# A two-layer transformer tower on one core: fp16 operands turned by DMA alone, three gathers for tile 1, new bank plan and new orders

## What is computed

```python
h = word_emb[ids] + pos_emb[pos] + type_emb[type];  h = layernorm(h) * gamma + beta
h = h + relu((performer(layernorm(h)) @ Wo.T + bo) @ Wfc.T + bfc)
h = h + prototype_ffn(layernorm(h))      # top 2 of 32, gates from distances
h = h + rope_attention(layernorm(h))     # causal, 16 heads of 16
h = h + relu(layernorm(h) @ Q(W1).T + b1) @ Q(W2).T + b2     # Q: ternary
```

## Time and profile before

| | us |
|---|---|
| three runs | 488.57, 484.67, 488.35 |
| median | 488.35 |
| profiled execution | 489.89 |
| its span | 488.2 |

### The profile page before, as it was taken

The page is one execution under the profiler, slowest core; times in us unless marked ns, Lnnn a source line. Parts: engine busy times, 40 slices in busy tenths (PEclk is TensorE's granted clock), DMA queues, the critical chain, the costliest instruction groups (busy, mean ns, idle before and its releaser), DMA issues.

```text
span 488.2 us, 11666 instructions
## 1 busy us (share of the span) xinstructions
PE 396.0 (81%) x3872; PEld 266.8 (55%) x3901; DVE 366.1 (75%) x1009; ACT 276.7 (57%) x589; POOL 246.4 (50%) x332
## 2 busy tenths in 40 slices
PE   3271757677868798999999988899999998898976
PEld 1140434435555556666666666666666675655634
DVE  4455488989788689889897879688978796765552
ACT  1223565254747385948585858485765747364531
POOL 6854226365747475757675657474654524342000
PEclk9775557589999899999999999999999999999999
...
GB/s 113 238 46 247 189 32 88 11 66 54 92 133 106 93 105 130 117 141 150 126 181 105 171 131 148 170 103 117 158 112 153 126 136 97 127 44 77 66 44 77
DMA packets 176860, 56.34 MB, mean 115 GB/s; under 512 B 168416, under 2 KB 174208, under 8 KB 176800
## 3 DMA queue, kind: packets, MB, share of 16 engines
...
## 4 chain that ended last, share of the span: by engine, by line
PE 32%; issue 13%; DVE 12%; DMA 11%; POOL 6%; ACT 5%; SPq 3%; DVEq 0%; ACTq 0%; POOLq 0%
PE PS L1322 9%; DMA hgT<-hgs 4%; PE PS L1751 3%; PE PS L1885 3%; PE PS L1619 3%; DMA qkT<-qs 3%; PE PS L1384 3%; DMA xTo<-xso 2%; PE PS L1867 2%; DVE split L989 1%; PE PS L1332 1%; DMA rTm<-split 1%; SPq L458 1%; PE PS L1333 1%; PE PS L1493 1%
## 5 line engine op out<-in xcount | busy, mean ns | idle before, releaser
L989 DVE TENSOR_REDUCE split<-PS 128x16 f16<-128x2048 f32 x16 | 36.7, 2297 | 7.9 <-PE PS L1716 7.8
L1332 PE MATMUL PS<-proj_hi,qkT 128*128 128x176 f16 x128 | 24.8, 256 | 18.7 <-DMA qkT<-qs 13.7
L588 POOL TENSOR_TENSOR stage_f<-stage_f 128x512 f32<-128x512 f32 x16 | 20.3, 1269 | 29.0 <-DVE stage_f L977 16.9
L581 POOL TENSOR_TENSOR rstdR<-rstdR,consts 128x1 f32<-128x1 f32 x16 | 8.7, 545 | 51.7 <-DVE rstdR L954 51.7
L1867 PE MATMUL PS<-w1q,xTM 128*128 128x512 f16 x128 | 32.9, 379 | 0.8 <-DVE xTM L1028 0.6
L1885 PE MATMUL PS<-w2q,mT 128*128 128x256 f16 x256 | 30.6, 273 | 1.7 <-ACT mT L1074 0.9
L1619 PE MATMUL PS<-faT_hi,hgT 128*128 128x256 f16 x128 | 26.2, 292 | 5.7 <-DMA hgT<-hgs 5.6
L1077 ACT ACTIVATE ehat<-esum,nmeanE,rstdE 128x256 f32<-128x256 f32 x16 | 9.5, 595 | 37.6 <-DVE nmeanE L770 22.0
L1885 PEld LDWEIGHTS PS<-w2q,mT 128*128 128x128 f16 x256 | 24.3, 98 | 6.0 <-issue 1.9
L1332 PEld LDWEIGHTS PS<-proj_hi,qkT 128*128 128x128 f16 x128 | 13.4, 105 | 24.2 <-DMA qkT<-qs 16.4
L598 POOL TENSOR_TENSOR rstdM<-rstdM,consts 128x1 f32<-128x1 f32 x16 | 8.8, 550 | 33.3 <-DVE rstdM L1016 33.3
...
## 6 DMA issues: line engine op xcount, KB each, us to landing
...
rT<-split SPq DMA_TRANSPOSE x26, 3.3
```

The lines of the kernel that those rows point to most:

```text
L588: g.tensor_tensor(rot[:, :, :].rearrange("p h d -> p (h d)"), rc[:, :], rs[:, :], ALU.add).then_inc(rot_ok, 1)
L989: v.tensor_reduce(slots(48)[:, 0:H, 0].rearrange("p (c j) -> p j c", j=4), PS[:, BANK["mk1"]:BANK["mk1"] + 4, :].rearrange("p j (c k) -> p ...
L1332: pe.matmul(dst, qkT[:, c0 + c, :], proj_hi[:, :], start=True, stop=False)
```

## The change

Six things change; the arithmetic of each product stays.

1. `BY_PE` shrinks from 28 turns to 7: `P` of tile 0, `o` of 0 and 15, `r` and `M` of 14 and 15. The 21 others go to `DMA_TRANSPOSE`: `o` of 1, 2, 14; `M` and `r` of 0, 1, 2, 13; `rT3.15`; `mT.15`; `rT1` and `rT2` of 0, 14, 15; `hgT` of 0 and 15. The operations of PE, ACT and DVE for fp16 turns (`rT1p`, `rT1a`, `rT1b` and so on) and the semaphore `turn_ok` are gone.
2. Tile 1 gathers from three tables like tile 0. `emb_type` becomes two buffers. The wait for the table `pt` moves from tile 1 to tile 2.
3. `load_w2` is issued behind `qp.0`.
4. New banks: `fQ` has 4 and 5, `fK` 0 and 1; `of`, `y`, `Rtr`, `rqk`, `rv` and `rot_` share bank 7.
5. Matmuls on nothing: one ahead of `m1.15`, six ahead of `m2.15` (the entry for `mk2` has no call that reads it).
6. All numbers of `START`, `STRETCH` and `PLACE` are new, and with them the order of each engine.

```diff
-START = (1.40537, 5.55987, 9.74075, 12.65258, 16.91573, 21.20954, 25.54553, 29.89477, 34.27529, 38.71698, 43.20261, 47.66727, 52.19494, 54.66439, 59.30117, 64.06203)
+START = (15.32428, 21.39685, 27.55784, 28.87087, 35.0305, 41.20738, 47.43255, 53.63816, 59.87893, 66.17932, 72.47996, 78.82444, 85.19901, 88.21914, 94.59957, 101.02611)
-    "sq": (-15.70252, -9.02388, -10.17824), "qT": (-20.94188, -17.2022, -20.19668), "diag": (-13.87668, -8.26036, -8.0608), "fK": (-14.33904, -9.0266, -9.06747),
+    "sq": (-38.70227, -21.84097, -23.62394), "qT": (-30.9939, -18.51016, -17.72932), "diag": (-32.59877, -16.74413, -15.51198), "fK": (-39.64337, -19.98461, -21.10499),
...
-    "qk": 6, "kmxT": 7, "kbc": 7, "fK": 0, "v": 7, "ctx": 2, "fQ": 0, "o": 3,
-    "of": 2, "Ftr": 7, "prt": 1, "fh": 0, "y": 7, "Rtr": 2, "rqk": 2, "rv": 1,
-    "mk1": 3, "pvx": 3, "pvT": 7, "wo": 0, "m1": 4, "m2": 2, "Ptr": 1, "ont": 2,
-    "Mtr": 4, "rot_": 7, "rT3p": 1, "mTp": 3, "rT1p": 0, "rT2p": 4, "hgTp": 6,
+    "qk": 2, "kmxT": 3, "kbc": 4, "fK": 0, "v": 6, "ctx": 3, "fQ": 4, "o": 2,
+    "of": 7, "Ftr": 6, "prt": 0, "fh": 1, "y": 7, "Rtr": 7, "rqk": 7, "rv": 7,
+    "mk1": 3, "pvx": 5, "pvT": 2, "wo": 2, "m1": 0, "m2": 2, "Ptr": 0, "ont": 3,
+    "rot_": 7, "Mtr": 1,
...
 WARM = {
-    "Rtr": {15: 1},
-    "Mtr": {14: 2},
+    "mk2": {15: 2},
     "m1": {15: 1},
-    "m2": {15: 1},
+    "m2": {15: 6},
 }
...
 BY_PE = {
-    "P": (0,), "o": (0, 1, 2, 14, 15), "M": (0, 1, 2, 13, 14, 15),
-    "r": (0, 1, 2, 13, 14, 15), "rT3": (15,), "mT": (15,),
-    "rT1": (0, 14, 15), "rT2": (0, 14, 15), "hgT": (0, 15),
+    "P": (0,), "o": (0, 15), "r": (14, 15),
+    "M": (14, 15),
 }
...
-TERN_BANK = 4
+TERN_BANK = 3
...
-        emb_type = sb("emb_type", [P, D])
+        emb_type = sb("emb_type", [P, 2, D])
...
                 if op == "PT":
...
-                    if t == 1:
-                        load_w2()
...
                     sp.dma_start_transpose(qpT[:, :, :], qe[:, :, :].rearrange("p j n -> p (j n)")).then_inc(qp_ok, 16)
+                    if t == 0:
+                        load_w2()
...
                 wait(g, e2_ok, t - RING + 1)
-                if t == 1:
+                if t == 2:
                     g.wait_ge(ids_ok, 4)
                     g.wait_ge(pt_out, 16)
...
-                          (emb_type[:, :], A["type"].rearrange("(r n) -> r n", n=D), ids[:, 2, t:t + 1]))
-                if t > 0:
+                          (emb_type[:, t % 2, :], A["type"].rearrange("(r n) -> r n", n=D), ids[:, 2, t:t + 1]))
+                if t > 1:
                     tables = (tables[0], (emb[:, slot, :], A["pt"], ids_pt[:, t:t + 1]))
...
-                    wait(g, g_ok[slot], 32 * (t // RING + 1) + (16 if slot == 0 else 0))
+                    wait(g, g_ok[slot], 32 * (t // RING + 1) + (16 if slot < 2 else 0))
+                    if t < 2:
+                        g.tensor_tensor(h_of(t), h_of(t), emb_type[:, t, :], ALU.add).then_inc(g_const, 1)
+                        wait(g, g_const, 24 + t)
                     wait(g, xn_ok["E"], t)
...
-                elif op == "rT1a":
-                    wait(a, turn_ok, TURNS["rT1p", t])
-                    wait(a, s2_ok, t)
-                    copy(rT[:, 0:HP, :][:, 0:4, :].rearrange("p c n -> p (c n)"), halves_of(BANK["rT1p"] + 0)[:, 0:4 * P]).then_inc(rT1_ok, 8)
...
-                elif op == "hgTp":
-                    wait(pe, hgl_ok, t + 1)
-                    wait(pe, gsl_ok, t + 1)
-                    wait(pe, hgh_ok, t + 1)
...
-                    for c in range(9):
-                        last = pe.transpose(halves_of(BANK["hgTp"] + c // 5)[:, c % 5 * P:(c % 5 + 1) * P],
-                                            hgs[:, c * P:(c + 1) * P], ident_h[:, :])
-                    last.then_inc(turn_ok, 1)
```

More of the change, by code:

```diff
@@ L131 @@
     "Ptr": "P", "Pe": "P", "PV": "P", "ont": "o", "oe": "o", "oV": "o",
[3 rows of a table removed]
-    "hgTp": "hgT", "hgTa": "hgT", "hgTb": "hgT",
+    "rot_": "r", "re": "r", "rV": "r", "Mtr": "M", "Me": "M", "MV": "M",
 }
@@ L158, in due @@
     return sorted(((op, t) for op in ENGINE[engine] for t in range(TILES) if taken(op, t)), key=lambda x: (place(*x), x[1]))
-TURNS = {x: n + 1 for n, x in enumerate(y for y in due("PE") if y[0] in ("rT3p", "mTp", "rT1p", "rT2p", "hgTp",))}
 def wait(eng, sem, count):
@@ L812, in step @@
                                            op0=ALU.add, op1=ALU.add).then_inc(qb_ok, 1)
+                elif op == "kmx":
+                    wait(v, fK_ok, t + 1)
+                    wait(v, kmxT_ok, t)
+                    v.tensor_reduce(by_bank(kmx), td(BANK["fK"]), AX_X, ALU.max).then_inc(kmx_ok, 1)
                 elif op == "qd":
@@ L930, in step @@
                         lower_rows("m", 1.0, 16)
-                elif op == "hgTb":
-                    wait(v, turn_ok, TURNS["hgTp", t])
-                    wait(v, y_ok, t)
-                    v.tensor_copy(hgT[:, :, :][:, 5:9, :].rearrange("p c n -> p (c n)"), halves_of(BANK["hgTp"] + 1)[:, 0:4 * P]).then_inc(hgT_ok, 8)
                 elif op == "ws":
@@ L1186, in step @@
                         setup_m()
+                elif op == "onh":
+                    wait(a, on_ok, t + 1)
+                    wait(a, T_ok["o"], 16 * t)
+                    copy(xs["o"][:, 0:D], onorm[:, :]).then_inc(hi_ok["o"], 1)
                 elif op == "Fxn":
@@ L1222, in step @@
                     copy(hgs[:, 0:R2], hg[:, :]).then_inc(hgh_ok, 1)
-                elif op == "hgTa":
-                    wait(a, turn_ok, TURNS["hgTp", t])
-                    wait(a, y_ok, t)
-                    copy(hgT[:, :, :][:, 0:5, :].rearrange("p c n -> p (c n)"), halves_of(BANK["hgTp"] + 0)[:, 0:5 * P]).then_inc(hgT_ok, 8)
                 elif op == "Rxn":
@@ L1242, in step @@
                     copy(slots(16), rot[:, :, :]).then_inc(rh1_ok, 1)
+                elif op == "rh3":
+                    wait(a, rot_ok, t + 1)
+                    wait(a, rT2_ok, 16 * t)
+                    copy(slots(48)[:, H:, :], rot[:, H:, :]).then_inc(rh3_ok, 1)
                 elif op == "rh2":
@@ L1541, in step @@
                     if t == 0:
+                        pe.wait_ge(T_ok["o"], 16)
                         ternary_means()
@@ new lines, in step @@
+                elif op == "rv":
+                    wait(pe, T_ok["R"], t + 1)
+                    free("vr_ok", vr_ok, t)
+                    free("rope_ok", rope_ok, 3 * issued["rqk"])
+                    free("T_r", T_ok["r"], 16 * issued["rot_"])
+                    free("T_R", T_ok["R"], issued["Rtr"])
+                    free("hF_ok", hF_ok, issued["y"])
+                    free("hP_ok", hP_ok, issued["of"])
+                    split_product(PS[:, BANK["rv"], 0:D], "R", "rwv").then_inc(rv_ok, 1)
+                    issued["rv"] = t + 1
```

557 lines of the change are left out of this document (173 added, 384 removed), and 50 rows, old and new, of tables (FOR_DMA, FOR_PE, PLACE).

## The result

| | before | after |
|---|---|---|
| median, us (lowest to highest) | 488.35 (484.67 to 488.57) | 494.99 (493.12 to 498.72) |
| profiled span, us | 488.2 | 495.4 |

The changed kernel is slower: the ratio is 1.0182, 95% interval 1.0147 to 1.0216. The forecast was 487, within 1%.

A forecast was written before the change was run, and what follows sets the result against it. PE was taken to bound the middle, DVE fK.0 to fK.3, dependent chains both ends. −5 + 2 − 1 + 0 − 1.5 + 4.1 = −1.4 us on 488.35 gave 487 (482 to 492; 8 in 10: 475 to 501).

The forecast's parts named there:

- Start, −5: Start to fK.0: w2's move −4, bank split −2.2, GpSimd's gathers +1, taken as −5 us (0 to −7).
- the −4 for w2: Start, wait for qT.0: w2 issued behind qp.0 saves 3.6 us of landing and 0.4 of queue.
- 0, if `kmx.0` meets other DVE work: Start: bound on the −2.2 us from fK.0 no longer waiting for qd.0; nothing won if DVE is otherwise occupied.
- GpSimd's +1: Start: two more gathers ahead of tile 0's Ers, less idle time, cost +1 us (0 to +2.5).
- I let 2 of the 5 us be lost: fK.0 to fK.3, bound by DVE: +2 us of the start's gain lost, net −3 at fK.3 (0 to −8).
- −1 to `y.3`: fK.3 to y.3: M and r turns of three tiles go from PE to DMA, −1 us (0 to −3).
- Steady part, 0: y.3 to fQ.15: same matmuls in another arrangement, 0 us (−10 to +6); wrong if tile spacing moves over 0.4 us.
- The wait on bank 7: Steady part: rv waits for three rope operations reading rqk in the shared bank; five matmul groups should hide it.
- fQ.15 to `y.15`, −1.5: Before y.15: shorter PE queue up to −3.9 us, hgT.15 by DMA +2, taken as −1.5 (−3.9 to +2).
- Tail, +4.1: y.15 to end: rT1/rT2 +2.1, rT3 +1.9, mT +2.1; raw sum +6.1, 2 us hidden: +4.1 (+2.1 to +6.1).
- The transposes are not hidden: Rival: tail +6.1 and hgT.15 +2 in full, start's gain eaten to −1: 495.5 us; chance 0.28.
- The clock falls for the last product: Rival, at m2.15: half clock costs +1.9 us on the middle case, 489; chance 0.1, part of the middle case's.

The follow-up runs named there:

- e4: The kernel before with only the load of w2 moved behind qp.0: 481.68 us, ratio 0.9906 to the kernel before.
- e3: The kernel before with only tile 15's five fp16 turns (hgT, rT1, rT2, rT3, mT) by DMA: 498.33 us, ratio 1.0221 to the kernel before.
- e1: The changed kernel with tile 15's five fp16 turns by PE, placed by hand, one matmul on nothing ahead of m2.15: 495.94 us, ratio 1.0166 to the kernel before.
- e11: e1 with rT1p, rT2p ahead of wo.13, rT3p behind mk2.15, s2.15 ahead of rot_.14: 494.06 us, ratio 1.0253 to the kernel before.
- e18: The kernel before with tile 0's fp16 turns (hgT.0, rT1.0, rT2.0) by DMA: 485.22 us, ratio 0.9984 to the kernel before.
- e9: The changed kernel with the load of w2 back behind PT.1: 494.34 us, ratio 1.0261 to the kernel before.
- e10: The changed kernel with fK.0 waiting for qd.0 again and kmx.0 behind qd.0: 497.83 us, ratio 1.0359 to the kernel before.
- e14: The changed kernel with five start entries moved: qmx.0, qb.0, kmx.0 on DVE, qT.1 on SP, v.1 on PE: 494.85 us, ratio 1.0154 to the kernel before.
- e8: The kernel before with only mT.15 turned by DMA: ratio 1.0067 to the kernel before.
- e17: e8 with six matmuls on nothing ahead of m2.15 in place of one: 488.86 us, ratio 1.0055 to the kernel before.

## Why the prediction was wrong

The forecast by stretch, and what the two profiles show, in us:

| | start to `fK.0` | to `fK.3` | to `y.3` | to `fQ.15` | to `y.15` | to the end | sum |
|---|---|---|---|---|---|---|---|
| forecast | −5 | +2 | −1 | 0 | −1.5 | +4.1 | −1.4 |
| measured | −6.6 | +7.6 | −4.8 | +2.4 | +2.5 | +6.1 | +7.2 |

Up to `y.3` the sum is right (−3.8 for −4), by luck: two misses of opposite sign. The 8.6 us between forecast and result lie behind it, and 6.0 of them in the last two stretches. The step that failed is the price of tile 15's turns by DMA, together with what I credited to PE's shorter queue against it. I had −1.5 and +4.1 for those two stretches, and they were +2.5 and +6.1.

*What bounds the kernel.* Right: PE in the middle, dependent chains at both ends, and nothing won in the middle.

*Start, −5.* Right in its mechanisms, and near in size up to `fQ.0` (−4.1 in the changed kernel, against the −4 for w2). With the bank split on top `fK.0` comes 6.6 us earlier, but `kd.0`, which all of tile 0 hangs on, only 2.8: my condition "0, if `kmx.0` meets other DVE work" came true in another form, since the list has DVE wait for GpSimd ahead of `qmx.0`. GpSimd's +1 was +1.4 on `Pxn.0`.

*"I let 2 of the 5 us be lost", −3 at `fK.3`.* Wrong. `e4` keeps the gain of w2 in the order of before, 0.94% of the time, so that DVE's work did not eat it there. In the changed kernel `fK.3` ended at 124.4, behind the 123 that I had named as the mark of error. I priced the new order by the waits it removes and not by the entries that now stand ahead of a ready instruction; the rows at `qmx.0` and `qT.1` show two such places, and what they are worth at the end is open.

*−1 to `y.3`.* This stretch gained 4.8, more than the 3 I allowed, and made up for the one ahead of it.

*Steady part, 0.* `y.3` to `y.15` went from 272.2 to 277.1 us, 23.1 a tile against 22.7, at the edge of the 0.4 that I had named; 3.0 of these 4.9 are `hgT.15`'s, and the rest is within the spread of single profiles. One piece is sure: `y.3` to `y.5` takes 51.6 us for 45.2 (48.7 to 51.9 in five profiles of the new order with its turns, 43.6 to 46.1 in those of the old one), so that the kernel was 2.6 us late at `y.5`. From there to `y.15` it takes 1.5 us less than before, and although `y.13` ends 7.3 us late, `y.14` is 3.7 and `y.15` 1.1 late. Of the +6.4 up to `y.5`, 3.6 are more idle time of PE, with these waits (us in total, times, longest) where before has 0.3 for `hgT` and none of the other two:

```profile
PE PS L1567 <- DMA rT<-split: 2.8, 2, 1.8
PE PS L1577 <- DMA rTm<-split: 2.2, 2, 1.9
PE PS L1508 <- DMA hgT<-hgs: 1.4, 1, 1.4
```

These turns go by DMA in both kernels; in the new order PE reaches their readers before they land. The other 2.8 are the same 447 matmuls taking longer, at half clock. PE's timeline in the changed kernel ahead of `y.5`:

```profile
209.80 0.62 PE L1567 MATMUL PS<-rT 48*128 48x128 f16 x16 [1.83 <-DMA rT<-split]
210.36 3.56 PE L1668 MATMUL PS<-w2q,mT 128*128 128x256 f16 x16
```

Sixteen matmuls that take 1.9 us take 3.56, behind a wait of 1.83 us for a turn by DMA. From 120 us to `y.15`, PE has some 10 us at the lower level in the changed kernel (near 171, 212 and 413 us) and 3.4 before (near 166); as an estimate from these, half of that is lost, 5.1 us against 1.7. The wait on bank 7 that I had looked for did not show.

*fQ.15 to `y.15`, −1.5.* It was +2.5. I had −3.9 from 4.3 us less queue on PE and +2 for `hgT.15`, taken together as −1.5. Up to `hgl.15` only 0.5 was won, and `hgT.15` cost +3.0. The turns that left PE were little gain, since PE was not short of time here: it idles 7.3 us of 49.2 where before has 4.0 of 46.7, and 1.9 of these are waits for `rTm`.

*Tail, +4.1.* It was +6.1, the top of its range, and at 54.5 us the stretch even lies inside the 50 to 55 that I had named as right; that mark was too wide to catch the miss. By term: `rT1`, `rT2` +2.0 (I had +2.1) and `mT` +2.2 (+2.1) are right. `rT3` is +3.5 (+1.9): I took the 3.23 us of tile 14 for its landing, and it was 4.82. Tile 15's rotary operations ahead of `rl.15` are +1.7, at nothing in my sum. That came in small pieces: `rqk.15` ends 0.5 us later, and its readers stand on DVE behind the reduction for tile 14 (L957, to 448.4) and among the operations of tile 14's output, which costs 0.8.

```profile
446.09 2.30 DVE L957 TENSOR_REDUCE split<-PS 128x16 f16<-128x2048 f32 x1
...
448.46 0.36 DVE L948 TENSOR_TENSOR stage_f<-PS,rope_sin 128x256 f32<-128x256 f32 x1
```

Against these +9.4, `s2.15` to the last input of `mT` took 3.1 us less, so that "2 us hidden" was not too much; with rounding that gives the +6.1. That this equals my raw sum is chance. In the order of before, `e3`, the turns of tile 15 by themselves cost 2.21%, so that they are enough for the sign there. That they are what costs in the new order too isn't shown: `e1` and `e11` turn them by PE and are no faster.

*The rivals.* "The transposes are not hidden" gave 495.5 against 494.99. Its tail (+6.1) and `hgT.15` (+2, measured +3.0) came out, but the number is in part luck: it had the start netting −1 where −3.8 was measured at `y.3`, and nothing for the stretches between. Its reason for the start (turns of tiles 0 to 2 by DMA eat the gain) is refuted by `e18` for three of the 11 turns, tile 0's fp16 ones in the order of before; the other eight were not tried. "The clock falls for the last product" did not happen in the profiled run of the changed kernel (1.92 us), but did in `e9`, `e10` and `e14`, which end in the same way, by 1.0 to 1.6 us, in `e8` and `e17`, and in the middle of the changed kernel, where I had not looked. The Trainium skill's page "TensorE: Matmul & The Clock Gate", section "Why this matters for your kernels", warns against idle gaps between bursts of matmuls because the clock drops. The traces agree that it can, after 2.41 us in `e17` (3.57 us for the last product), and show that it need not, after 2.43 us in the changed kernel (1.92).

*What stays open.* What the new order costs by itself, without the turns: `e1`, `e11` put the turns back and are still 1.7% and 2.5% slower than before, but at places picked by hand, at which `rl.15` to `s1.15` takes 7.4 us. Why `rTm.15` takes 4.8 us in the new order. What tile 13's late `y` costs. And what decides whether six matmuls on nothing keep the clock.
